# Casting two weight matrices by column blocks and in another order, and waiting for each block where it is read

## The reference

```
xn = layernorm(x)
# branch 1
n  = layernorm(xn) * gamma + beta
z, gate = split(n @ W_in.T)                  # W_in 8192 x 2048
y  = z * sigmoid(clip(z)) * softmax(-dt) * silu(clip(gate))
attn = y @ W_out.T + xn                      # W_out 2048 x 4096
# branch 2, weights int32, (w - 128) * scale per row
h  = silu(xn @ Wg.T) * (xn @ Wu.T)           # 8192 x 2048 each
ffn = h @ Wd.T                               # 2048 x 8192
out = x + attn + ffn
```

## Time and profile before

| | us |
|---|---|
| median of 13 runs | 10100.87 |
| lowest and highest of them | 9702.5 and 11383.65 |
| profiled execution | 9743.22 |
| its span on core 6, the slowest | 9741.4 |
| its span on the fastest core | 9669.8 |

### The profile page before, as it was taken

The page is one execution under the profiler, slowest core; times in us unless marked ns, Lnnn a source line. Parts: engine busy times, 40 slices in busy tenths (PEclk is TensorE's granted clock), DMA queues, the critical chain, the costliest instruction groups (busy, mean ns, idle before and its releaser), DMA issues.

```text
span 9741.4 us, 87853 instructions; the slowest of 8 cores (9669.8 to 9741.4 us)
## 1 busy us (share of the span) xinstructions
PE 8132.7 (83%) x36864; PEld 3631.5 (37%) x36864; DVE 2074.9 (21%) x1678; ACT 2119.7 (22%) x1420; POOL 832.5 (9%) x813
## 2 busy tenths in 40 slices
PE   0000488999999788999999888999999888999998
PEld 0000133444444333444444333444444333444443
DVE  0065311211111222111112211111112212111112
ACT  0022000133333100133332100233332100233332
POOL 0000000011111000011111000011111000111110
PEclk9999999999999899999999899999999999999999
DMA  9933565487776863487787753587787733677776
GB/s 115 126 120 130 111 144 100 80 80 78 76 75 73 153 144 69 78 82 75 76 78 87 155 126 65 84 78 76 74 77 90 134 82 67 84 77 75 76 74 103
DMA packets 2334962, 911.85 MB, mean 94 GB/s; under 512 B 2001249, under 2 KB 2263409, under 8 KB 2328945
## 3 DMA queue, kind: packets, MB, share of 16 engines
q0 software_dynamic: 1325728, 453.07, 46.9%
q1 hardware_dynamic: 837586, 293.75, 13.5%
q10 hardware_dynamic: 171264, 159.42, 6.4%
HBM read 1224.86 MB, written 151.01 MB: 141 GB/s over the span
## 4 chain that ended last, share of the span: by engine, by line
PE 79%; DMA 6%; DVE 2%; issue 2%; ACTq 0%; SPq 0%; ACT 0%; DVEq 0%; POOL 0%; POOLq 0%
PE psZ L646 17%; PE psG L646 17%; PE psZ L588 9%; PE psOa L675 8%; PE psOb L675 8%; PE psG L588 8%; PE psOa L616 5%; PE psOb L616 4%; DMA xnck<-xnT_scr 2%; DMA xbuf<-x_scr 2%; DMA w1r<-wi_bf 1%; PE psOa L646 1%; PE psOb L646 1%; DVE actB L937 1%; DMA w2r<-wo_bf 0%
## 5 line engine op out<-in xcount | busy, mean ns | idle before, releaser
L588 PE MATMUL psZ<-xnslot,w1r 128*128 128x512 bf16 x3968 | 947.8, 400 | 1453.3 <-DMA w1r<-wi_bf 1127.9
L646 PE MATMUL psZ<-xnslot,gur 128*128 128x512 bf16 x7680 | 1741.4, 386 | 3.7 <-ACT gur L870 2.2
L646 PE MATMUL psG<-xnslot,gur 128*128 128x512 bf16 x7680 | 1696.8, 379 | 0.0
L870 ACT ACTIVATE gur<-gur 128x2048 bf16<-128x2048 bf16 x512 | 976.2, 1909 | 3134.4 <-DMA gur<-wuT 3033.5
L588 PEld LDWEIGHTS psZ<-xnslot,w1r 128*128 128x128 bf16 x3968 | 397.0, 102 | 2002.7 <-issue 1615.9
L646 PEld LDWEIGHTS psZ<-xnslot,gur 128*128 128x128 bf16 x7680 | 761.4, 99 | 945.8 <-issue 149.3
L646 PEld LDWEIGHTS psG<-xnslot,gur 128*128 128x128 bf16 x7680 | 751.0, 98 | 906.6
L748 POOL DMA_DIRECT2D gur<-wuT x256 | 293.6, 1147 | 7284.0 <-PE psG L646 7100.4
L588 PE MATMUL psG<-xnslot,w1r 128*128 128x512 bf16 x3968 | 877.2, 379 | 0.0
L880 ACT ACTIVATE wdr<-wdr 128x2048 bf16<-128x2048 bf16 x256 | 488.9, 1910 | 668.0 <-DVE sum_ac L909 450.7
L820 ACT ACTIVATE szcb<-psZ 128x1024 bf16<-128x1024 f32 x124 | 126.7, 1022 | 2291.8 <-PE psG L588 2275.6
(11 more groups left out here) (77 smaller groups left out, 4353.8 us busy)
## 6 DMA issues: line engine op xcount, KB each, us to landing
gur<-wgT POOLq DMA_DIRECT2D x256, 512.0 KB, 15.6
gur<-wuT POOLq DMA_DIRECT2D x256, 512.0 KB, 11.0
w1r<-wi_bf SPq DMA_DIRECT2D x256, 512.0 KB, 6.1
wdr<-wdT POOLq DMA_DIRECT2D x256, 512.0 KB, 12.2
w2r<-wo_bf SPq DMA_DIRECT2D x256, 256.0 KB, 5.4
wi_bf<-w_inT POOLq DMA_DIRECT2D x4, 8192.0 KB, 202.9
gx<-x_td SPq DMA_DIRECT2D x32, 1024.0 KB, 74.9
xtck<-x_dt ACTq DMA_DIRECT2D x64, 512.0 KB, 5.1
```

What stands on the lines that cost most here:

```text
L588: e.matmul(ps[:, th * TH:(th + 1) * TH], w1r[:, sl * 2048 + dc * 128: sl * 2048 + (dc + 1) * 128], xnslot[:, dc * TILE + th * TH: dc * TIL ...
L646: e.matmul(ps[:, th * TH:(th + 1) * TH], gur[:, sl * 2048 + dc * 128: sl * 2048 + (dc + 1) * 128], xnslot[:, dc * TILE + th * TH: dc * TIL ...
L870: M.do(lambda e, buf=buf: e.activation(buf, buf, AF.Copy, bias=-128.0), c_ac, ("guc", t, c) if nn % 2 == 1 else None)
```

## The change

The casts are listed once in `CASTS`. `W_in` is cut into four blocks of 2048 columns (all 2048 rows each), not into four blocks of 512 whole rows. `W_out` stays in four blocks of 1024 whole rows. The order is columns 0 to 2047, columns 4096 to 6143, `W_out` block 0, the two other column blocks, and the rest of `W_out`. Each cast has a semaphore of its own (existing ones that nothing else used). The wait for all casts at the end of the prologue is gone; in the first tile SP waits ahead of every w1 or w2 load for the block that it reads.

```
+        wi_cast_sem = [s_wl["wi"][0], s_wl["wi"][1],
+                       s_wl["wg"][0], s_wl["wg"][1]]
+        wo_cast_sem = [s_wl["wu"][0], s_wl["wu"][1],
+                       s_wl["wd"][0], s_wl["wd"][1]]
+        def wi_cast(b):
+            return (wi_cast_sem[b], ("wic", b),
+                    wi_bf[:, 2048 * b:2048 * (b + 1)],
+                    w_inT[:, 2048 * b:2048 * (b + 1)])
+        def wo_cast(s):
+            return (wo_cast_sem[s], ("woc", s),
+                    wo_bf[1024 * s:1024 * (s + 1), :],
+                    w_outT[1024 * s:1024 * (s + 1), :])
+        CASTS = [wi_cast(0), wi_cast(2), wo_cast(0), wi_cast(1), wi_cast(3),
+                 wo_cast(1), wo_cast(2), wo_cast(3)]
...
             def pro_gpsimd(M):
-                for rs in range(4):
-                    M.do(lambda e, rs=rs: e.dma_start(
-                        wi_bf[512 * rs:512 * (rs + 1), :],
-                        w_inT[512 * rs:512 * (rs + 1), :]),
-                        s_wil, ("wi", rs))
-                for rs in range(4):
-                    M.do(lambda e, rs=rs: e.dma_start(
-                        wo_bf[1024 * rs:1024 * (rs + 1), :],
-                        w_outT[1024 * rs:1024 * (rs + 1), :]),
-                        s_wil, ("wo", rs))
+                for ctr, key, dst, src in CASTS:
+                    M.do(lambda e, dst=dst, src=src: e.dma_start(dst, src),
+                         ctr, key)
...
                 M.waitv(s_dtw, s_dtw.v)
-                M.waitv(s_wil, s_wil.v)
...
                             chunk = (n // 2) if n % 2 == 0 else 32 + n // 2
+                            if tt == 0:
+                                blk = (chunk // 16 if chunk < 32
+                                       else 2 + (chunk - 32) // 16)
+                                M.wait(wi_cast_sem[blk], ("wic", blk))
...
                         q, dc = n // 16, n % 16
+                        if tt == 0:
+                            M.wait(wo_cast_sem[q], ("woc", q))
```

More of the change, by code:

```diff
@@ L339, in pro_sync @@
                     M.wait(s_dtw, ("dtw", "pm", 31))
-                    M.wait(s_wil, ("wo", 3))
+                    for ctr, key, _, _ in CASTS:
+                        M.wait(ctr, key)
                     for nm, src in pairs:
```

## The result

Against the kernel before, the changed kernel's time stands at a ratio of 0.9913 (95% interval 0.9885 to 0.9941), so it is 0.9% faster. Forecast was 9666 / 9743.2 = 0.9921. The profiled execution took 9627.35 us (span 9625.6, core 0), where the forecast for one like it was 9666. The median over all its 11 runs is 10310.57 us, and that of before, over 50 runs, 10309.72: in more than half of the executions of either kernel the cores of one die or both were granted a lower TensorE clock and took longer (in the changed kernel's execution of 10926.8 us cores 4 to 7 ran at 0.85 and took 10879 to 10925 us, cores 0 to 3 at 0.98 and took 9593 to 9626), which says nothing about the change. That median lies outside the stated range of 9555 to 9850, and so did the median of before.

What follows compares the result with a forecast made beforehand. Prologue bound by the layernorm chain, its loads waiting on cast packets. Casts' end 551 plus 51 for transposes plus 358 gives 960 against 1039.6: 79 less 2 for waits, 77 off 9743.2, is 9666 us; range 9555 to 9850.

Steps and rivals of the forecast that it cites:

- The removed wait is worth 0: GpSimd's prologue end: the casts are not what is waited for, so removing their wait alone gains 0.
- One packet for one packet: SP's queue against the casts: each SP packet waits for one cast packet, 4.28 us; turns are single records.
- Small packet at 0.586 us: W_in casts: a packet of 4 KB written costs 0.586 us of an engine, range 0.38 to 0.64.
- rival (a): Small cast packets cost less, 0.38 us: casts end at 446, gain 182, time 9561 us; chance 0.10.
- (c): Narrow rows make casts slow; at double cost they end at 851, time 9965 us; chance 0.13 at double.
- Start near 100 us: Layernorm chain on ScalarE: first group of x lands, and first statistics begin, near 100 us instead of 483.
- The x2 stores of group 0 end near 325: SP's queue in the prologue: the eight x2 stores, interrupted by the first W_out cast, end near 325 us.
- Two or three transposes before the casts' end: SP's queue: two or three pass before casts end near 551 us, some 50 us apiece, one over 100.
- 13 transposes at 3.96 us, 51 us: SP's queue behind the casts' end: the 13 transposes left take 51 us, to 602 us.
- The prologue's end at 960, 79 us earlier: Barrier before the steady part: falls at 960 us against 1039.6, 79 us earlier.
- The added waits, 2 us over nine pairs of panels: First tile's w1 loads on SP: added waits never block, some 0.1 us each, 2 us lost.
- The absolute time: Whole kernel: 9666 us, from the profiled 9743.2 less 77, for an execution like the profiled one.

Runs made afterwards that it cites:

- experiment 1: Kernel before, its row blocks and cast order kept, only the wait for all casts moved from GpSimd's prologue end to SP ahead of the first w1 load; ratio 1.0003.
- experiment 2: Changed kernel with the wait for all eight casts put back at GpSimd's prologue end; profiled execution 9983.4 us, no ratio, barrier at 973.7 us on core 0.
- experiments 3 and 4: 3: changed kernel with W_in in two blocks of 4096 columns, 0.9938; 4: changed kernel with group 2's loads and group 1's stores ahead of the sixteen transposes, 0.9816.

## Why the prediction was right or wrong

- **The removed wait is worth 0.** Right: experiment 1 (1.0003), and in experiment 2 putting it back moves the barrier by 3 us on core 0 and 5 in the mean.
- **One packet for one packet.** Right, and it is the mechanism of the change: 1008 to 1002 before; 1710 to 1658 and 934 to 933 with packets of 4 KB; 1131 to 1133 with 8 KB. That the turns are single records, as the prediction says, wasn't shown by its equal sums but is by the 16 and 16 in 5 us above. Packets of 4, 8 and 32 KB put the first statistics at 90, 145 and 483 us.
- **Small packet at 0.586 us.** Right: 0.52 us at the start, and 451 us of engine time over the whole cast phase, where 450 was put in. Neither rival (a), 446 us for the casts' end, nor (c), 851, came: they end near 556, where 551 was forecast. The Trainium skill ("DMA: Bandwidth & Descriptors", "Latency and other measured facts") reports copies at 103 GB/s with rows 4 MiB apart and at 207 with rows 512 KiB apart. No such loss is seen here, the casts moving the same bytes in the same engine time; whether the engines did read 4 MiB apart, as the prediction assumed, no run shows.
- **Start near 100 us.** 90.
- **The x2 stores of group 0 end near 325.** The terms given add up to 332 (240 + 54 + 38); 336.5 was measured.
- **Two or three transposes before the casts' end.** Three, of 50, 87 and 83 us (50 apiece and one over 100 were expected). The second met long packets in its last 25 us, the third throughout. It did end with the casts, as forecast, but was issued only 83 us ahead of their end and so didn't reach 100.
- **13 transposes at 3.96 us, 51 us.** 54.8 us (556.84 to 611.62); the last one was expected at 602.
- **358 us from there.** 358.8.
- **The prologue's end at 960, 79 us earlier.** 970.4, 69 us earlier on these two cores, 72 in the mean of eight. Of the 10 us missing, 5 are the casts' end and 4 the transposes behind it. Up to 556 us SP's queue took 0.194 x 556 = 108 us of the engines, where 73 + 21 + 6 + 1 = 101 were put in; the casts' own 450 us were right.
- **The added waits, 2 us over nine pairs of panels.** Hardly seen. The first matmul comes 48.7 us after the barrier before and 47.6 after, the one on the second panel 20.9 us behind it before and 21.0 after. (These lines also show the 1088 us that the prediction reads from the earlier trace rows, which end at 1039.6.)

```profile
1088.30 9.22 PE L588 MATMUL psZ<-xnslot,w1r 128*128 128x512 bf16 x32 [1088.30 <-DMA w1r<-wi_bf]
...
1017.99 9.04 PE L599 MATMUL psZ<-xnslot,w1r 128*128 128x512 bf16 x32 [1017.99 <-DMA w1r<-wi_bf]
```

- **The absolute time.** This step failed: the base of the sum, 9743.2 us, with the range of 9555 to 9850 built round it. Apart from the 2 us of waits the sum changes only the prologue, and it puts the granted clock behind it at nothing. The runs show a median of 10309.7 us for the kernel before and 10310.6 for the changed one: the base lay 566 us below the median of before, and the prologue's gain is 72. The listed median, 10100.9, already said that half of the executions take 3.7% more than the base or worse; the prediction names it, and still gives its range for an execution like the profiled one. The same term shows at a smaller size in the forecast of such an execution. The sum took core 6, 8701.8 us of steady part at a clock of 0.97, as what a steady part takes ("about 8702"). After, it was 8655.2 at 0.98. So the profiled execution came 39 us below the forecast (9627 against 9666) though the prologue gained 69 us and not the 77 put in: 46.6 us is the difference of the steady parts, and by cores 0 to 3 above it comes from the clock and not from the change.
- **The ratio.** 0.9921 has held (0.9885 to 0.9941): the gain divided by the base hardly feels that the base is wrong.

The chances were 0.55 for the forecast's own range, 9625 to 9700, which does hold the profiled execution, though only by 2 us, and with a steady part that was shorter for its clock; and 0.67 for faster, which came.

## What to carry to other kernels

When two DMA queues have work, look at packets and not at bytes: if their numbers in a window are equal, the queue with the small packets waits for one large packet of the other at each turn, and cutting the other's rows shorter gives it its share; here, down to 4 KB, at no cost in bandwidth. Then ask what the earlier start meets: here 393 us of earlier start were worth 72, since a strictly serial run of small-packet transposes stood in the chain until the bulk transfer ended, and moving it behind, with the next loads ahead of it, gave 105 us more. A sum of engine work up to the end of the bulk transfer, plus the chain that is left behind it, forecast the prologue to within 11 us (960 against 970). With that known, the variants of experiments 3 and 4 were expected at 976 and 857 and came at 979 and 866.

And don't build an absolute time on one profiled execution: here the median of the same kernel lay 566 us above it and the effect was 72, so that the ratio could be forecast from one profile and the time couldn't.

## What the runs showed of the hardware

The turns between the queues go packet by packet whether the cast's packets carry 4, 8 or 32 KB (934 to 933, 1131 to 1133, 1008 to 1002; 16 to 16 in 5 us). A cast from DRAM to DRAM costs the same engine time when the two thirds of it that are `W_in` go in pieces of 4 KB written (8 KB read every 32 KB) as in contiguous pieces of 32 KB: 451 and 450 us of 16 engines. With casts and loads both waiting the changed kernel's core 0 moved 172 GB/s in the first 100 us, counted as written, against 120 up to 483 us before; the share of `x` loads in these bytes differs (10.1 of 17.2 MB now).
